# Loads of x issued later in each slot, with the clearing DMA and the loads regrouped on the sync queue

## What is computed

```python
def reference(x, cls_tok, ...):
    # tokenizer: patches of 4 x 4 pixels, 8 heads
    q  = _ln(patch_means) @ Wq.T                  # one query per patch
    kv = _ln(pixels) @ Wkv.T                      # 16 keys and values per patch
    attn = softmax(einsum('bhpd,bhpnd->bhpn', q * scale, k))
    h = patch_means + einsum('bhpn,bhpnd->bhpd', attn, v) @ proj_w.T + proj_b
    h = concatenate([cls_tok, h], axis=1)
    # recurrence: x_in's first axis is the step
    h = h + scan(tanh(xp_t + h_prev @ W_hh.T))(layernorm(h))
    # experts: top 2 of 8 per token, gelu MLP of width 256
    h = h + moe(layernorm(h))
    return h
```

## Time and profile before

| | us |
|---|---|
| median of 3 runs | 1443.71 (1442.06 to 1451.28) |
| the profiled execution | 1444.4 |
| its span | 1442.5 |

### The profile page before, as it was taken

The page is one execution under the profiler, slowest core; times in us unless marked ns, Lnnn a source line. Parts: engine busy times, 40 slices in busy tenths (PEclk is TensorE's granted clock), DMA queues, the critical chain, the costliest instruction groups (busy, mean ns, idle before and its releaser), DMA issues. The chain is left out here.

```text
span 1442.5 us, 61906 instructions
## 1 busy us (share of the span) xinstructions
PE 1314.1 (91%) x25169; PEld 1072.3 (74%) x25169; DVE 1031.0 (71%) x2724; ACT 816.2 (57%) x1999; POOL 711.9 (49%) x852
## 2 busy tenths in 40 slices
PE   5799999999999999999999999999996999999970
PEld 3577777777878778777777777777775889877850
DVE  4676777676777777787877767678856676588874
ACT  1455655665556555655555555555556777655640
POOL 1344343443434344443366666564431577776476
PEclk8999999999999999999999999999998999999995
DMA  8999989998989989998999999999643688899897
GB/s 274 406 317 307 312 293 305 302 307 279 303 293 314 304 292 298 301 304 280 302 337 327 344 330 351 318 338 324 221 138 110 215 280 290 279 323 343 278 291 221
DMA packets 186614, 423.70 MB, mean 294 GB/s; under 512 B 23968, under 2 KB 89312, under 8 KB 186208
## 3 DMA queue, kind: packets, MB, share of 16 engines
q1 hardware_dynamic: 170336, 380.27, 77.8%
q0 software_dynamic: 14048, 38.16, 8.2%
q10 hardware_dynamic: 1952, 1.32, 0.4%
HBM read 332.26 MB, written 87.39 MB: 291 GB/s over the span
## 5 line engine op out<-in xcount | busy, mean ns | idle before, releaser
L1132 DVE BATCH_NORM_STATS2 st<-xp 128x6 f32<-128x512 f32 x512 | 340.2, 696 | 15.0 <-DMA xp<-xpix 14.5
L672 POOL TENSOR_TENSOR rs_px<-px_ve,half_neg 128x16 f32<-128x16 f32 x64 | 187.0, 2921 | 177.5 <-DVE px_ve L1137 177.5
L786 ACT ACTIVATE zT<-bank 128x512 f32<-128x512 f32 x256 | 138.6, 597 | 85.6 <-PE bank L975 85.6
L779 ACT ACTIVATE z_s<-bank 128x512 f32<-128x512 f32 x256 | 138.7, 597 | 79.5 <-PE bank L965 79.5
L934 PE MATMUL bank<-xc,u 128*32 128x64 f32 x8192 | 148.5, 220 | 26.4 <-issue 25.5
L934 PEld LDWEIGHTS bank<-xc,u 128*32 128x32 f32 x8192 | 130.8, 110 | 53.2 <-issue 42.4
L760 ACT ACTIVATE u<-bank 128x512 f32<-128x512 f32 x256 | 132.1, 603 | 48.7 <-PE bank L913 48.7
L1421 POOL DMA_INDIRECT y<-ys_dram,slot x130 | 127.7, 982 | 60.9 <-issue 36.9
L657 POOL TENSOR_TENSOR q_rs<-q_ve,half_neg 128x1 f32<-128x1 f32 x64 | 35.1, 548 | 243.7 <-DVE q_ve L1149 243.7
L975 PE MATMUL bank<-ident,z_s 128*128 128x128 f32 x1024 | 150.0, 280 | 2.7 <-ACT z_s L779 1.6
L413 POOL DMA_INDIRECT xs_dram<-xrow,slot x130 | 130.7, 1006 | 37.1 <-issue 34.5
(11 more groups left out here) (178 smaller groups left out, 3145.4 us busy)
## 6 DMA issues: line engine op xcount, KB each, us to landing
xp<-xpix SPq DMA_DIRECT2D x256, 512.0 KB, 4.8
xc<-xg SPq DMA_DIRECT2D x256, 512.0 KB
xc<-xs_dram SPq DMA_DIRECT2D x86, 256.0 KB, 4.7
ys_dram<-y_s SPq DMA_DIRECT2D x86, 256.0 KB, 3.9
xs_dram<-zero SPq DMA_DIRECT2D x57, 384.0 KB, 5.5
base_dram<-h SPq DMA_DIRECT2D x65, 128.0 KB, 5.7
rows_dram<-tok SPq DMA_DIRECT2D x65, 128.0 KB, 5.5
hb<-base_dram SPq DMA_DIRECT2D x65, 128.0 KB, 4.6
```

The source lines that it names most:

```text
L672: pool.tensor_tensor(rs_px[:, :], px_ve[:, :], half_neg[:, :], ALU.pow).then_inc(s["px_done"], 1)
L779: act.activation(z_s[:, r, 2 * half:2 * half + 2, :].rearrange("p a c -> p (a c)"), BIG[2 * r + half][:, :], ACT.Copy).then_inc(s["z_done" ...
L786: act.activation(zT[:, c, :, :].rearrange("p h (a r t) -> p r h a t", r=2, t=TS)[:, r, :, :, :], BIG[f][:, :].rearrange("p (a h t) -> p h ...
L1132: dve.bn_stats(st[:, j, :], xp[u.x][:, 2 * j:2 * j + 2, :].rearrange("p i c -> p c i")).then_inc(s["st_done"], 1)
```

## The change

Only SyncE's program of a slot is rewritten. No DMA is added or taken away, and no engine's work changes but the order and the semaphores on which SyncE waits before it issues.

```diff
                 if more_xp:
                     wait(sp, s["z_ps"], w, 2, 2)
+                    wait(sp, s["s_ps"], v, 1, 1)
                     load_xp(sp, w.x, w.k + XBUF, [0])
-                    wait(sp, s["rT_ps"], u, 1, 1)
+                    wait(sp, s["zt_ps"], w, 4, 4)
                     load_xp(sp, w.x, w.k + XBUF, [1])
-                    wait(sp, s["zt_ps"], w, 4, 2)
+                    wait(sp, s["c_ps"], v, 1, 1)
                     load_xp(sp, w.x, w.k + XBUF, [2])
-                    wait(sp, s["rn_ps"], u, 1, 1)
+                    wait(sp, s["q_ps"], u, 1, 1)
                     load_xp(sp, w.x, w.k + XBUF, [3])
                 for q in scatter_now(u.k)[1:]:
                     load_row(sp, q)
-                if mid and 0 <= u.k - 2 < len(pieces):
-                    wait(sp, s["c_ps"], v, 1, 1)
-                    clear_rows(sp, u.k - 2)
                 if more_xc:
                     wait(sp, s["s_ps"], v, 1, 1)
-                    wait(sp, s["q_ps"], u, 1, 1)
+                    if back:
+                        wait(sp, s["a_ps"], w, 1, 1)
                     load_xc(sp, v.c, v.k + XC, [0])
+                    wait(sp, s["u_ps"], u, 1, 1)
+                    load_xc(sp, v.c, v.k + XC, [1])
                 if late:
                     keep_base(sp, t)
                     keep_row(sp, t)
                 if more_xc:
-                    if back:
-                        wait(sp, s["a_ps"], w, 1, 1)
-                    load_xc(sp, v.c, v.k + XC, [1])
-                    wait(sp, s["u_ps"], u, 1, 1)
+                    if end:
+                        wait(sp, s["h_ps"], z, 1, 1)
                     load_xc(sp, v.c, v.k + XC, [2])
+                if mid and 0 <= u.k - 2 < len(pieces):
                     if back:
                         wait(sp, s["pj_ps"], w, 1, 1)
+                    clear_rows(sp, u.k - 2)
+                if more_xc:
+                    if end:
+                        wait(sp, s["ht_ps"], z, 1, 1)
                     load_xc(sp, v.c, v.k + XC, [3])
```

More of the change, by code:

```diff
@@ L591, in slot @@
             def slot(sp, u, front, mid, back, end, late):
-                v, w, t = u.before(), u.before(2), u.k - 4
+                v, w, z, t = u.before(), u.before(2), u.before(3), u.k - 4
                 more_xp, more_xc = back and w.k + XBUF < UNITS, mid and v.k + XC < UNITS
```

## The result

| | before | after |
|---|---|---|
| median us | 1446.22 (1442.06 to 1451.28, 4 runs) | 1500.15 (1490.79 to 1513.18, 4 runs) |
| span of the profiled execution | 1442.5 | 1495.6 |

The changed kernel is slower: ratio 1.0351, 95% interval 1.0311 to 1.0392. 1467 us was forecast, and the time lies inside the range of 1436 to 1510. The direction was right. The loss, 51 to 54 us, is more than double the 23 us of the sum; by its size it falls to the rival called much slower (over 1490), which was given 0.13. One of the changed kernel's four runs, 1513.18 us, was a slow execution and isn't in the ratio; without it the loss is 51 us.

What follows compares the result with a forecast made beforehand. TensorE was taken to bound the kernel, with instruction blocks delayed behind x data. 2.9 us a round times 11 is 32, cut to 24 for the last 20 slots, net +23 on 1444.4: 1467 us, range 1436 to 1510.

Steps and rivals of the forecast that it cites:

- the sum: Token stage, 55 slots: delays of late instruction blocks added up by request position, net +23 us on 1444.4, giving 1467 us.
- the rival called much slower: Instruction fetches queue behind all data that is issued: +75 us, 1519 us; chance 0.13 for over 1490.
- What bounds the kernel: TensorE sets the slot of 15.88 us; 36 us over 55 slots come from instruction blocks delayed behind x data.
- The tail: Slot's start: data of the slot before still flows until 3.4 to 5.2 us in, taken as 3.6.
- the hole: Stretch of about 3 us before 6.9 us into a slot in which the data queues are empty.
- Nothing else waits: Later landings of x loads, zeros and token rows cost nothing, having slack; loads coming late: under 2 in 100.
- A round: Five slots with 14 request positions, five of which matter: +2.9 us each time, times 11 makes 32 us.
- The last third: Stage's last 20 slots: delays taken as full already from breaks of up to 2.5 us, so loss counted at a third.
- the discount: Counting the stage's last 20 slots at a third, which lowers the loss from 32 to 24 us.
- The rule of turns between queues: DMA engines go round the queues, so a fetch waits about one turn of the data queue; loss near zero.

## Why the prediction was right or wrong

**What bounds the kernel: right.** The breaks before "issue" are TensorE's instruction blocks behind x data. All 75 of over 0.3 us in the token stage of the two kernels end at the same count modulo 256, and with the data cut to about a third they fall from 25.5 us to 1.6.

**The tail: right in place and length.** 3.4 to 5.2 us into the next slot was forecast, the hole until 6.9. The windows show 278 GB/s until 4 us, a hole from 4 to 6, and 250 GB/s from 6. The sum went by 3.6 us, below the 4.3 to 5.2 that its own full queues give.

**Nothing else waits: right** for `xp` and `xc` behind the first 45 us, and for the stores. GpSimd's wait for rows is new and off the path.

**The sum: wrong in size.** From the lengths of the slots 7 to 36 over 15.88 us, by the position at which the block was requested (mean of 6 slots each; before, after, gain of the sum):

| requested | before | after | measured | forecast |
|---|---|---|---|---|
| 14 us in | 0.92 | 0.97 | +0.05 | 0 |
| 15.7 | 0.19 | 0.63 | +0.4 | +0.3 |
| slot's start | 0.01 | 1.36 | +1.35 | +1.2 |
| 1.3 | 0.34 | 2.15 | +1.8 | +1.1 |
| 12.8 | 0.44 | 0.88 | +0.4 (+1.05 in four of the six) | +0.3 |

A round costs 4.1 us instead of 2.9. The last line is small only because the kernel before has one slot of 2.6 us among its six. Two causes. One: the delays themselves. Blocks requested at the slot's start waited 3.3 us for their packet instead of 1.0, those of 1.3 us in 2.8 instead of 1.1, those of 13 to 15 us in 3.4 instead of 1.3. The 2.9 us that the sum took from the earlier trace rows were about right for a full queue, but it put the kernel before at 1.5 in the second case and the change of the third at 0.3. The other: the clock. In the token stage it stood at 1.2 GHz in one place before (3.4 us) and in six after (20.5 us in sum), five of them in the last 20 slots. Each follows a break of 1.86 us or more, but six of 1.89 to 2.22 us were followed by none. The longest break, a piece of work behind it, and the windows, where the granted clock shows a mean of 0.76 and 0.78 (two levels, 2.4 and 1.2 GHz):

```profile
579.70 0.42 PE L938 MATMUL bank<-xc,u 128*32 128x64 f32 x13 [2.57 <-issue]
...
582.38 0.66 PE L948 MATMUL bank<-sm,pick 128*32 128x128 f32 x8
```

```profile
578.00:582.00 4.00, 2.30 (x22) 2.21 (x22) 1.83 (x4) 0.37 (x2) 0.96 (x2) 0.76 0.17 33
582.00:585.40 3.40, 3.40 (x53) 2.43 (x51) 1.60 (x5) 1.92 (x7) 0.32 (x1) 0.78 0.85 261
```

The same fold (L944, now L948) takes 0.66 us there instead of 0.43. By an estimate from these stretches, 17 us more at half the clock, this is most of the 10.6 us by which the matmuls are busy longer, and the sum had no term for it.

**The last third: the step that failed most.** The sum counted its 20 slots at a third, 4 us, since the longest breaks of before (2.5 us) were taken to say that delays were full there. They cost 22.2 us. In those slots rows are fetched and scattered beside x, 342 GB/s instead of 304 over 100 us before, and so the bunch lasts longer. The windows of the slot that starts at 836 show no hole in its first 6 us:

```profile
836.33:840.30 3.97, 3.97 (x119) 2.97 (x111) 2.23 (x7) 2.15 (x6) 2.93 (x4) 1.00 1.04 398
840.30:841.30 1.00, 1.00 (x54) 0.91 (x54) 0.96 (x5) 0.35 (x1) 0.37 (x1) 1.00 1.06 415
841.30:842.30 1.00, 1.00 (x10) 0.97 (x10) 0.97 (x5) 0.19 (x1) 0.55 (x1) 1.00 0.90 353
```

One break of 2.5 us was read as the state of a whole stretch; the discount had no row for a typical delay there. The mean time from request to packet in those slots was 2.5 us before and is 2.9 now, so the delays were not full yet. The matmuls' breaks before "issue" grew there from 12.9 to 28.2 us, and the work got 7.3 us longer, mostly by the lower clock. Without the discount the sum would have been 32 us, with the measured round 45.

**Luck.** 1500 us lies near the rival called much slower, but not by its mechanism: that blocks wait for all that is issued is what the run with everything issued at once speaks against.

**The rule of turns between queues**, by which the sum would have been zero, is not borne out as "one turn, whatever stands behind": the same block in the same slot makes TensorE stand 0.47 us or 1.61 us, by nothing but the place of the data. But the delay does level off at 3 to 4 us, so it isn't the whole queue that is waited for either.

**What stays open.** Why the delay levels off, and what the number of DMAs and the DMA engine that carries a packet do to it; and why some breaks of 2 us bring the clock down and others don't. The bunch issued at once has 12 us of breaks more, but less time at the lower clock (13.7 us against 20.5), and its time doesn't stand apart from the changed kernel's. No version here beats the kernel before; its quarters, spread one by one over the slot, are the best of the eleven orders and sizes of a full load that ran.

## What to carry to other kernels

When TensorE stands before "issue" in the middle of a run of equal instructions, look at what the data queues hold: instructions come through the same DMA engines, and breaks that end at the same count modulo 256 give them away. Spreading loads evenly over the slot was worth more here than keeping any one part of it free, since a quiet stretch on the issuing queue only bunches the same bytes elsewhere, and they arrive 2 us later and run on for as long as their volume takes. Price small bounded stalls by their number and place, stretch by stretch, and don't take one long stall for the state of a whole stretch. For breaks of about 2 us and more, add the slower clock that can follow.

## What the runs showed of the hardware

- A load over 64 partitions moved 257 GB/s with full queues, one over 128 partitions 402 GB/s, at the same 4 KB rows. Halving every load of x by partitions cost 11% of the kernel.
- TensorE's breaks before "issue" in the scores go with the DMA volume and with how it is bunched: 1.6 us at 1.75 MB a slot, 25.5 at 4.9 MB spread, 27.9 at 3.85 MB bunched, 68.2 at 4.9 MB bunched, 94.2 at 4.9 MB with slow transfers.
- An instruction block's packet came 0.2 us after its request at the slot's start with 1.75 MB a slot, 1.4 us in the kernel before, and 3 to 4 us with over 1.5 MB in the queue. With 3 MB it was no later than with 2.
- A break of 2.57 us in TensorE was followed by a stretch of lower granted clock (mean 0.76 to 0.78 over 7.4 us), in a part of the stage that else shows 1.00. All six low stretches of the changed kernel's token stage follow breaks of 1.86 us or more; six more of 1.89 to 2.22 us had none.
